# Attention's end in a four-part transformer kernel: column sums, late decay weights, the last residual, the block's close

## The chip, the cores and the metric

One NeuronCore of a Trainium2 chip runs the whole program in one launch. The metric is device time of the program in microseconds (us), the median of several executions. The engines are named as in the profile: PE (TensorE, matmul) with PEld (its weight loads), DVE (VectorE), ACT (ScalarE), POOL (GpSimd) and SP (SyncE, which only issues DMAs here). "PEclk" is the granted clock of PE: 1.00 is 2.4 GHz, 0.50 is 1.2 GHz.

## What is computed

The reference has four residual steps over `x` of 4 x 512 x 512 (16 tiles of 128 tokens), float32:

1. `x += tanh(g0) * attention(layernorm(x), ctx, ctx)`, eight heads, scores and softmax over the context;
2. `x += tanh(g) * mixture of 8 experts, 2 per token` (gate, up with 512 columns, down);
3. `x += tanh(g) * layernorm(x + summary)`, where `summary` is the mean over time of a linear recurrence over the context: `s_t = K s_(t-1) + W_in c_t + b_in`, then `W_out s + b_out`, with `K = sigmoid(decay)`. Since all of it is linear, the kernel weights each context row with a scalar (the decay weights, one per position, from a scan of 512 numbers), sums the rows per batch (`u`, 512 numbers for each of 4 batches), and multiplies by `W_in` and later `W_out`;
4. `x += tanh(g) * mixture of 64 experts, 4 per token, and two shared experts`.

The change is about the end of step 1, where `u` is also summed, and about the first lines of step 2.

## The kernel before, in words

The program consists of four blocks, one after the other; between two blocks all engines meet. `attention` is the first, `mixture0` the second. Within a block each engine has its own instruction stream, in program order, and semaphores tie them.

**Attention** runs a software pipeline over tiles (`steps`): step `i` does the scores of tile `i` in four quarters `b`, the rough maxima of tile `i+1` (bank `pM`), the attention output and residual of tile `i-1`, the gate logits of tile `i-2` (`xnT`, `wg`) and the places of tile `i-3` in its experts' tables (`positions`: PE L578, L579; `place`: DVE). The first and last steps are unrolled. For tile `i-1` the relay is: value matmuls (PE L543), copies of the sums `attn` (ACT L639, L640), reciprocals (DVE L754), product with `numer` (POOL L448), a `pool.drain()`, residual add into `x_sb` (POOL L450), statistics (DVE L769), scale factors (POOL L462 to L469), normalised tile `xn` (ACT L665), transposes (PE L603), `xnT` (ACT L648), gate logits (PE L609), the two largest and `mask` (DVE L708 to L723), positions, slots (DVE L737), scatter into the table `tab0` (POOL L426, indirect DMA).

**Decay weights.** In the first step DVE makes the scan `crow` (`state_weights`, L686), PE turns it to columns (L485, eight records for four matmuls) and flips it (L488), DVE copies it (`ccol`) and makes `wsel` (L695), weights of 4 columns per tile. PE waits for all that ahead of its first rough score. **Context sum.** For each of 16 context tiles one matmul has `wsel` (4 columns) as weights and 512 columns of context moving: `u` comes out as a row for each batch (`pM[0:4]`). The tiles are spread over steps 16 to 18 (L496); after the last, ACT copies the row (L671), PE turns it to columns (L517), ACT copies it to `ucol` (L673). Tiles 4 to 15 share one semaphore, so PE waits at tile 4 for all twelve loads, which SP issues (L358) when the last scores are done (`qk_done`). `W_in` (`win`, L369) comes behind them.

**Tail.** After the last place PE counts (L503), DVE makes the padding rows (`padrow`, L790), a table of tiles per expert (`tinfo`), then the rows of results (`take0`, L818 to L828) and the bias (`bin_col`). Eight padding writes of zeros, 256 KB each, go out after `padrow`: four by SP, two by ACT (L301), two by POOL (L432, indirect). The block closes with GpSimd's drain, as blocks do by default.

**Mixture 0.** SP waits for all zeroing, padding and scattering, reads the first row of a tile from `tinfo` and issues `m_x` (L900). PE first projects `ucol` by `W_in` in row form (L990: weights of 4 columns, 512 moving), DVE copies the row, PE turns it (L985), and DVE adds the bias into `mstate` (L1063), read only by the third block. Then, per expert tile: transposes (L949), ACT rounds (L1017), DVE makes the low part (L1059), PE multiplies up (L956, high and low parts: three matmuls for each block), and so on through ACT, DVE and POOL splits of the weights (L1002, L1044, L935).

Of the kernel before, what the change touches and what calls it, by code (L numbers as in the profile page):

```python
# [8 lines left out]
I32 = mybir.dt.int32  # L9
# [5 lines left out]
P = 128  # L15
# [20 lines left out]
SUMS = 2  # L36
AT_ONCE = 1
# [38 lines left out]
def build(nc, A, out):  # L76
    ctx = ExitStack()
    with ctx:
# [28 lines left out]
        chosen1 = sb("chosen1", [P, E1], BF16)  # L107

# [10 lines left out]
        with arena0:  # L119
# [4 lines left out]
            s_padded_too = ctx.enter_context(nc.semaphore("table0_padded_too"))  # L124
# [46 lines left out]
def attention(nc, A, T):  # L171
# [6 lines left out]
    with c:  # L178
# [41 lines left out]
        flip = xnT[:, 0, :]  # L220
# [3 lines left out]
        crow = attn[0:1, :]  # L224
        wsel = sb("wsel", [P, B, TPB, B])
        urow = sb("urow", [B, D])

        padf, padrow = sb("padf", [P, E0]), sb("padrow", [P, E0], I32)
        cnt, ntf, nti = sb("cnt", [P, E0]), sb("ntf", [P, E0]), sb("nti", [P, E0], I32)
# [3 lines left out]
        usum = sb("usum", [P, 4 * TILES])  # L233
        big = sb("big", [P, L0_TILES * E0])
        past = big[0:1, 0:L0_TILES * E0].rearrange("p (t e) -> p t e", e=E0)
        slots = usum[:, 2 * TILES:4 * TILES]
# [16 lines left out]
        ctx_loaded = [sem(f"ctx_loaded_{n}") for n in range(2)]  # L253
# [18 lines left out]
        wsel_ready = sem("wsel_ready")  # L272
        urow_ready, uT_full = sem("urow_ready"), sem("uT_full")

        block = c.enter_context(nc.Block())
# [28 lines left out]
        def _(sp):  # L304
# [68 lines left out]
        def _(pool):  # L373
# [8 lines left out]
            nc.gpsimd.memset(flip, 0.0)  # L382
            nc.gpsimd.memset(ones[:], 1.0)
            nc.gpsimd.memset(invt[:], 1.0 / SEQ)
            nc.gpsimd.memset(wsel[:], 0.0)
# [9 lines left out]
            nc.gpsimd.affine_select(flip, flip, [[1, P]], ALU.not_equal, 1.0, base=1 - P, channel_multiplier=1)  # L395
# [25 lines left out]
            for i in range(-3, TILES + 3):  # L421
# [57 lines left out]
        def _(pe):  # L479
# [3 lines left out]
            pe.wait_ge(crow_ready, 1)  # L483
            for j in range(TPB):
                last = nc.tensor.matmul(pM[:, j:j + 1], crow[0:1, j * P:j * P + P], ones[0:1, 0:1], start=True, stop=True)  # L485
            last.then_inc(col_full, 1)
            pe.wait_ge(col_ready, 1)
            nc.tensor.matmul(pM[:, 0:TPB], flip, ccol[:, 0, :], start=True, stop=True).then_inc(col_full, 1)  # L488
            pe.wait_ge(wsel_ready, 1)
# [17 lines left out]
            def weights_sum():  # L507

                for j in range(TPB):
# [4 lines left out]
            def context_columns():  # L514
                pe.wait_ge(urow_ready, 1)
                for n in range(DB):
                    last = nc.tensor.transpose(pM[:, n * B:n * B + B], urow[:, n * P:n * P + P], ident[0:B, 0:B])  # L517
                last.then_inc(uT_full, 1)
# [34 lines left out]
            def step(i, u, odd):  # L553
                s, o = odd, 1 - odd
                if valid(i):
                    need(pe, q_split, i + 1)
                    need(pe, k_lo_ready, i + 1)
                for b in range(4):
                    if valid(i):
                        scores(i, s, b)  # L560

# [13 lines left out]
                    if b == 0 and valid(i - 3):  # L575

                        need(pe, mask_ready, i - 2)
                        nc.tensor.matmul(pT[:, 0:E0], before[:], mask[:, o, :], start=True, stop=False)  # L578
                        nc.tensor.matmul(pT[:, 0:E0], onesb[:], chosen[:, o, :], start=False,  # L579
                                         stop=True).then_inc(pos_full, 1)  # L580
                        if isinstance(i, int) and i == TILES + 1:
                            weights_sum()
                            weighted_context(range(6, 9))
# [7 lines left out]
                    if isinstance(i, int) and (i, b) == (TILES, 1):  # L591
                        weighted_context(range(0, 2))
                    if isinstance(i, int) and (i, b) == (TILES, 3):
                        weighted_context(range(2, 6))
                    if isinstance(i, int) and (i, b) == (TILES + 1, 1):
                        weighted_context(range(9, 10))
# [1639 lines left out]
```

## Time and profile before

| | us |
|---|---|
| median of 3 runs | 1121.69 (1120.41 to 1123.66) |
| profiled execution, its own time | 1124.97 |
| its span in the profile | 1123.2 |
| attention, up to the meeting of the engines | about 0 to 324 |
| mixture 0 | about 324 to 533 |
| mean granted clock of PE | 0.967 |

Busy shares over the span: PE 92%, PEld 66%, DVE 64%, POOL 52%, ACT 45%. They are means over very different stages: in the last 30 us of attention no engine is busy throughout. In a row of the timeline, the first number is the start, the second the time from the start of the group to its end; the bracket is the idle time of the engine before it and what ended it. A float32 matmul appears as two MATMUL records, a float32 transpose as one. A row with "SPq" or "ACTq" is the issuing of DMAs, not their transfer.

### The profile page before, as it was taken

The numbers are of one execution on the slowest core, as the hardware profiler recorded it, in microseconds if no ns is written. First come the engines' busy times: TensorE is split into PE (matmuls) and PEld (weight loads), VectorE is DVE, ScalarE is ACT, GpSimd is POOL, SyncE is SP. The second block draws the span as 40 slices with busy tenths as digits, with TensorE's granted clock in tenths as the row PEclk, the third lists the DMA queues.
The fourth block names the chain that finished last, engine by engine and source line by source line (L and its number), as shares of the span: only waits on it lengthen the run. The fifth ranks groups of instructions, "written<-read, shape, count | busy, mean of one in ns | idle before, by whom it ended". The sixth has DMA issues, their size and how long they took to land. (4 is left out here: it accounts for less than half of the span.)

```text
span 1123.2 us, 18838 instructions
## 1 busy us (share of the span) xinstructions
PE 1028.6 (92%) x5364; PEld 739.4 (66%) x5364; DVE 723.4 (64%) x1703; ACT 500.6 (45%) x880; POOL 589.3 (52%) x556
## 2 busy tenths in 40 slices
PE   5899999999869999998899999999989999999950
PEld 3456555565327777775289478577768888888840
DVE  4577787876448888886688248267316666666650
ACT  3466566565338888886432201311313333333320
POOL 6466766775416676675534646356432344333541
PEclk8999999999989999999899999999999999999985
DMA  9976555773544332332540241043269999999638
GB/s 289 342 228 201 171 180 191 240 246 104 197 150 152 111 105 102 112 103 75 181 144 20 87 140 44 11 136 112 87 209 345 333 323 313 277 331 336 160 70 149
DMA packets 128254, 199.49 MB, mean 178 GB/s; under 512 B 35975, under 2 KB 44167, under 8 KB 128186
## 3 DMA queue, kind: packets, MB, share of 16 engines
q1 hardware_dynamic: 106538, 160.66, 42.7%
q0 software_dynamic: 21360, 37.48, 13.2%
q8 instruction: 32, 0.52, 0.2%
q10 hardware_dynamic: 288, 0.52, 0.1%
q14 instruction: 36, 0.29, 0.1%
HBM read 133.10 MB, written 87.56 MB: 196 GB/s over the span
## 5 line engine op out<-in xcount | busy, mean ns | idle before, releaser
L935 POOL TENSOR_TENSOR m_down_lo<-wo,m_down_hi 128x512 fp32r<-128x512 f32 x78 | 129.8, 1683 | 74.9 <-ACT m_down_hi L1030 74.9
L543 PE MATMUL bank<-win,vT 128*128 128x512 f32 x256 | 124.5, 600 | 0.0
L703 DVE TENSOR_REDUCE negmax<-bank 128x1 bf16<-128x512 f32 x128 | 85.6, 672 | 43.2 <-PE bank L550 42.8
L633 ACT ACTIVATE win<-bank 128x512 f32<-128x512 f32 x128 | 69.4, 594 | 90.1 <-PE bank L535 86.3
L1044 DVE TENSOR_TENSOR m_up_lo<-w,m_up_hi 128x1024 fp32r<-128x1024 f32 x78 | 96.8, 1242 | 13.1 <-ACT m_up_hi L1002 11.8
L2034 POOL DMA_INDIRECT out<-m_y,m_token x32 | 50.9, 1590 | 91.2 <-DMA out<-m_y,m_token 61.5
L1264 POOL DMA_INDIRECT tab<-stage_up,slot x64 | 65.9, 1029 | 53.4 <-DVE slot L1610 35.5
L2064 PE MATMUL bank<-y,m_w 128*128 128x128 f32 x736 | 89.7, 275 | 0.0
L2178 ACT ACTIVATE sh_gate_a<-bank 128x512 f32<-128x512 f32 (+1 forms) x40 | 20.5, 513 | 150.8 <-PE bank L2171 120.6
L2034 POOL DMA_INDIRECT sums<-m_y,m_token x32 | 51.2, 1599 | 69.2 <-DVE m_y L2128 41.3
L2064 PEld LDWEIGHTS bank<-y,m_w 128*128 128x128 f32 x736 | 86.4, 193 | 0.1
L2171 PE MATMUL bank<-flat_hi,w_hi 128*128 128x512 f32 (+1 forms) x320 | 74.4, 355 | 2.4 <-DVE flat_lo L1677 1.6
L550 PE MATMUL bank<-k_hi,q_parts 128*128 128x512 f32 x128 | 68.9, 549 | 7.7 <-issue 2.9
L2082 PE MATMUL bank<-split_space,m_h_hi 128*128 128x512 f32 x128 | 73.7, 576 | 1.9 <-DVE split_space L2114 1.9
L2171 PE MATMUL bank<-flat_lo,w_hi 128*128 128x512 f32 (+1 forms) x320 | 73.2, 350 | 1.6 <-issue 1.6
L2171 PE MATMUL bank<-flat_hi,w_lo 128*128 128x512 f32 (+1 forms) x320 | 71.9, 347 | 0.0
L956 PE MATMUL bank<-m_up_hi,m_xT_hi 128*128 128x512 f32 x156 | 67.7, 434 | 2.8 <-DVE m_up_lo L1044 2.6
L2092 ACT COPY y<-bank 128x512 f32<-128x512 f32 x64 | 37.4, 587 | 73.4 <-PE bank L2056 64.7
L543 PEld LDWEIGHTS bank<-win,vT 128*128 128x128 f32 x256 | 47.8, 192 | 27.1 <-issue 18.9
L754 DVE RECIPROCAL attn<-attn 128x128 f32<-128x128 f32 (+1 forms) x48 | 58.5, 1220 | 6.6 <-ACT attn L640 2.6
L956 PE MATMUL bank<-m_up_lo,m_xT_hi 128*128 128x512 f32 x156 | 61.6, 395 | 0.0
L956 PE MATMUL bank<-m_up_hi,m_xT_lo 128*128 128x512 f32 x156 | 61.3, 393 | 0.0
(297 smaller groups left out, 2503.9 us busy)
## 6 DMA issues: line engine op xcount, KB each, us to landing
tab<-zeros SPq DMA_DIRECT2D x16, 1056.0 KB
m_w<-in_L_ffn_Wg SPq DMA_DIRECT2D x46, 256.0 KB
m_w<-in_L_ffn_Wu SPq DMA_DIRECT2D x46, 256.0 KB
m_w<-in_L_ffn_Wd SPq DMA_DIRECT2D x46, 256.0 KB
m_x<-tab SPq DMA_DIRECT2D x39, 256.0 KB, 2.6
ytab<-m_y SPq DMA_DIRECT2D x39, 256.0 KB, 2.1
stage_up<-tab SPq DMA_DIRECT2D x32, 264.0 KB
m_x<-tab SPq DMA_DIRECT2D x32, 264.0 KB
```

What stands on the lines that cost most here:

```text
L543: nc.tensor.matmul(pO[s * 2 + h][:], vT[:, s, sb_, h:h + 2, :].rearrange("p a c -> p (a c)"), probs[:, sb_ % 2, h, :], start=(sb_ == 0), s ...
L550: nc.tensor.matmul(rough_bank(k, m)[:], q_parts[:, s, h, t * P:t * P + P], k_hi[:, s, h, :], start=True, stop=True).then_inc(pm_full, 1)
L633: nc.scalar.activation(probs[:, b % 2, h, :], pS[h][:], ACT.Exp, scale=1.0 / HEAD).then_inc(p_ready, 1)
L703: nc.vector.tensor_reduce(negmax[:, s, m:m + 1], rough_bank(k, m)[:], AX.X, ALU.max, negate=True).then_inc(pm_read, 1)
L935: nc.gpsimd.tensor_tensor(dn_lo[:, m, :], row(wo0, e * MB + m), dn_hi[:, m, :], ALU.subtract).then_inc(dn_lo_ready, 1)
L956: last = nc.tensor.matmul(pH[s][:], x[:, s, d, :], w[:, d, :], start=(d == 0 and part == 0), stop=(d == DB - 1 and part == 2))
L1044: nc.vector.tensor_tensor(up_lo[:, at, :], blocks(w01, e * DB + half * HALF, HALF), up_hi[:, at, :], ALU.subtract).then_inc(up_lo_ready, 1)
L1264: nc.gpsimd.indirect_dma_start(T["tab1"], bass.IndirectOffsetOnAxis(slot1[:, j, k:k + 1], 0), flat[:, j, :], None, bounds_check=E1 * CAP1 ...
L2034: nc.gpsimd.indirect_dma_start(tables[e % SUMS], bass.IndirectOffsetOnAxis(token[:, e % META:e % META + 1], 0), y[:, e % RING, :], None, b ...
L2064: last = nc.tensor.matmul(pH[s][:, k * CAP1:(k + 1) * CAP1], w[:, b, :], xT[:, s, b, :], start=(b == 0), stop=(b == DB - 1))
L2082: last = nc.tensor.matmul(pY[o][:], a[:, o, :], w[:, o, :], start=(part == 0), stop=(part == 2))
L2171: last = nc.tensor.matmul(out, w[:, k, wc], x[:, d, cols], start=(d == 0 and part == 0), stop=(d == DB - 1 and part == 2))
```

## The change

- The decay weights are made late: the scan (`state_weights`) at the end of DVE's step 14, the turning on PE in step 15 (`decay_column` behind the scores of quarter 1, `turned_column` behind the scores of quarter 3, each ahead of that quarter's value matmuls), the copies at the end of DVE's step 15 (`decay_columns`). `wsel` goes.
- The context is the stationary operand: for each context tile four pairs of 128-column weights and one moving column `ccol`, into columns of `pM`, so `u` comes out as columns. Loads are waited for four tiles at a time. The order over the last steps is 0-1, 2-7, 8, 9-10, 11-15 where it was 0-1, 2-5, 6-8, 9, 10-12, 13-15; `weights_sum` stands before tile 0; `positions` comes first in its quarter in the late steps.
- The projection by `W_in` is done in columns too (`project`): output columns 0 and 1 at the end of attention, 2 and 3 at the start of mixture 0. The copy and the transposes between go.
- The residual of tile 15 is added by DVE; POOL signals after its product, without a drain.
- POOL's two padding writes go to ACT, behind its copy of `ucol`; all eight count on one semaphore. The block is closed with `no_gpsimd_drain=True`.
- `take0` is computed at the end of mixture 0's DVE stream, `bin_col` ahead of the last `place`.

```diff
-        block = c.enter_context(nc.Block())
+        block = c.enter_context(nc.Block(no_gpsimd_drain=True))
...
-                    sp.dma_start(ctx_at[t], c_v[:, t, :]).then_inc(ctx_loaded[min(n, 1)], 16)
+                    sp.dma_start(ctx_at[t], c_v[:, t, :]).then_inc(ctx_loaded[n], 16)
...
-                if i == TILES + 2:
-                    pool.wait_ge(pad_ready, 1)
-                    for e in range(6, E0):
-                        nc.gpsimd.indirect_dma_start(T["tab0"], bass.IndirectOffsetOnAxis(padrow[:, e:e + 1], 0),
-                                                     zeros[:, 0:D], None).then_inc(T["s_padded_too"], 16)
...
-                        nc.gpsimd.tensor_tensor(attn[:, cols_], attn[:, cols_], numer[:, cols_], ALU.mult)
-                    pool.drain()
-                    nc.gpsimd.tensor_tensor(x_sb[:, i - 1, :], x_sb[:, i - 1, :], attn[:],
-                                            ALU.add).then_inc(x1_ready, 1)
+                        last = nc.gpsimd.tensor_tensor(attn[:, cols_], attn[:, cols_], numer[:, cols_], ALU.mult)
+                    if i == TILES:
+                        last.then_inc(x1_ready, 1)
+                    else:
+                        pool.drain()
+                        nc.gpsimd.tensor_tensor(x_sb[:, i - 1, :], x_sb[:, i - 1, :], attn[:],
+                                                ALU.add).then_inc(x1_ready, 1)
...
+            def turned_column():
+
+                pe.wait_ge(col_ready, 1)
+                nc.tensor.matmul(pM[:, 0:TPB], flip[:], ccol[:, 0, :], start=True, stop=True).then_inc(col_full, 1)
...
-                    if t in (0, 4):
-                        pe.wait_ge(ctx_loaded[t // 4], 16 * (TILES - 4) if t else 64)
-                    last = nc.tensor.matmul(pM[0:B, :], wsel[:, t // TPB, t % TPB, :], ctx_at[t],
-                                            start=(t == 0), stop=(t == TILES - 1))
+                    if t % 4 == 0:
+                        pe.wait_ge(ctx_loaded[t // 4], 64)
+                    for n in range(DB):
+                        at = n * B + t // TPB
+                        last = nc.tensor.matmul(pM[:, at:at + 1], ctx_at[t][:, n * P:n * P + P],
+                                                ccol[:, 1, t % TPB:t % TPB + 1],
+                                                start=(t == 0 and n == 0), stop=(t == TILES - 1 and n == DB - 1))
...
+                late = isinstance(i, int) and i >= TILES
                 for b in range(4):
                     if valid(i):
                         scores(i, s, b)
+                    if late and b == 0 and valid(i - 3):
+                        positions(i, o)
+                    if isinstance(i, int) and (i, b) == (TILES - 1, 1):
+                        decay_column()
+                    if isinstance(i, int) and (i, b) == (TILES - 1, 3):
+                        turned_column()
...
-            weighted_context(range(13, TILES))
-            context_columns()
+            weighted_context(range(11, TILES))
+            first_projections()
...
-            nc.scalar.copy(urow[:], pM[0:B, :]).then_inc(urow_ready, 1)
-            act.wait_ge(uT_full, 1)
-            nc.scalar.copy(ucol[:].rearrange("p n b -> p (n b)"), pM[:, 0:DB * B])
+            nc.scalar.copy(ucol[:].rearrange("p n b -> p (n b)"), pM[:, 0:DB * B]).then_inc(T["ucol_ready"], 1)
+            pad(act, range(6, 8))
...
+                            if isinstance(i, int) and i == TILES:
+                                nc.vector.tensor_tensor(x_sb[:, i - 1, :], x_sb[:, i - 1, :], attn[:], ALU.add)
+                                dve.drain()
...
-                if isinstance(i, int) and i == -3:
+                if isinstance(i, int) and i == TILES - 2:
                     state_weights()
+                if isinstance(i, int) and i == TILES - 1:
+                    decay_columns()
...
+def project(nc, T, columns):
+
+    out, win, ucol = T["bank"][6], T["win"], T["ucol"]
+    for m in columns:
+        for n in range(DB):
+            last = nc.tensor.matmul(out[:, m * B:m * B + B], win[:, n, m * P:m * P + P], ucol[:, n, :],
+                                    start=(n == 0), stop=(n == DB - 1))
+    return last
...
-            pe.wait_ge(T["s_win"], 16)
-            for n in range(DB):
-                last = nc.tensor.matmul(pY[0][0:B, :], ucol[:, n, :], winT[:, n, :], start=(n == 0), stop=(n == DB - 1))
-            last.then_inc(mrow_full, 1)
+            project(nc, T, range(EARLY_COLUMNS, DB)).then_inc(mstate_full, 1)
```

## Rows read from the trace of the kernel before

**Rows 1.** section 1 of the page: engine, busy us (share) x instructions

```profile
PE 1028.6 (92%) x5364; PEld 739.4 (66%) x5364; DVE 723.4 (64%) x1703; ACT 500.6 (45%) x880; POOL 589.3 (52%) x556
```

**Rows 2.** timeline, start: us, length, engine line op out<-in xcount [idle before <-releaser]

```profile
7.92 1.23 DVE L686 TENSOR_TENSOR_SCAN attn<-kdec,invt 1x512 f32<-1x512 f32 x1
...
9.29 1.83 PE L485 MATMUL bank<-ones,attn 1*128 1x1 f32 x8 [9.29 <-DVE attn L686]
...
13.98 4.12 PE L550 MATMUL bank<-k_hi,q_parts 128*128 128x512 f32 x8 [2.01 <-DVE wsel L695]
...
41.93 1.14 ACT L659 CAST k_hi<-wout 128x512 fp32r<-128x512 f32 x2 [5.63 <-DMA wout<-in_ctx]
```

**Rows 3.** timeline, last full steps of attention

```profile
279.25 0.17 DVE L729 TENSOR_TENSOR rows<-bank,base 128x8 f32<-128x8 f32 x1 [1.21 <-PE bank L579]
...
288.58 3.65 PE L543 MATMUL bank<-win,vT 128*128 128x512 f32 x8
...
289.91 0.17 DVE L723 TENSOR_TENSOR mask<-onehot 128x8 bf16<-128x8 f32 x1
```

**Rows 4.** timeline, the relay after the last value matmul

```profile
293.53 3.83 DVE L754 RECIPROCAL attn<-attn 128x256 f32<-128x256 f32 x3 [0.33 <-ACT attn L640]
...
298.94 0.17 DVE L723 TENSOR_TENSOR mask<-onehot 128x8 bf16<-128x8 f32 x1
...
301.83 1.26 POOL L450 TENSOR_TENSOR x_sb<-x_sb,attn 128x512 f32<-128x512 f32 x1 [3.68 <-issue]
...
303.19 0.69 DVE L769 BATCH_NORM_STATS2 bn<-x_sb 128x6 f32<-128x512 f32 x1 [4.09 <-POOL x_sb L450]
...
305.63 0.81 ACT L665 ACTIVATE xn<-x_sb,ln 128x512 f32<-128x512 f32 x1 [10.25 <-POOL ln L469]
...
308.47 0.66 PE L603 MATMUL bank<-ident,xn 128*128 128x128 f32 x4
...
313.67 0.18 PE L578 MATMUL bank<-mask,before 128*128 128x8 bf16 x1
...
315.35 0.17 DVE L790 CAST padrow<-padf 128x8 int32<-128x8 f32 x1
```

**Rows 5.** timeline from pads to first expert matmul; landing of L900

```profile
316.49 4.69 SPq L301 DMA_DIRECT2D tab<-zeros  x4
...
324.94 6.52 SPq L900 DMA_DIRECT2D m_x<-tab  x5
...
329.73 0.66 PE L949 MATMUL bank<-ident,m_x 128*128 128x128 f32 x4
...
331.78 0.50 PE L956 MATMUL bank<-m_up_hi,m_xT_hi 128*128 128x512 f32 x1 [0.22 <-DVE m_xT_lo L1059]
...
DMA to landing us min/median/max: 2.5/2.8/3.0
```

**Rows 6.** windows: length, busy by engine, PEclk, DMA share, GB/s

```profile
323.50:324.00 0.50, 0.00 (x0) 0.00 (x0) 0.00 (x0) 0.00 (x0) 0.00 (x0) 0.50 0.43 156
...
324.00:330.00 6.00, 5.95 (x10) 1.12 (x11) 2.53 (x3) 3.48 (x4) 0.37 (x4) 0.63 0.49 147
```

**Rows 7.** timeline, one-column records (L510) and row-form context (L496)

```profile
304.81 0.97 PEld L510 LDWEIGHTS bank<-ones,ccol 128*128 128x128 f32 x8
...
305.80 2.74 PE L496 MATMUL bank<-ctx_late,wsel 128*4 128x512 f32 x6
```

**Rows 8.** chain of waits, experts: start, length, what

```profile
844.02 3.57 PE bank L2064 x16
...
848.07 1.79 PE bank L2064 x16
```

**Rows 9.** windows, before the end of the first mixture

```profile
529.00:530.00 1.00, 0.90 (x3) 0.49 (x3) 0.00 (x0) 0.00 (x0) 0.05 (x1) 0.90 0.21 78
```

**Rows 10.** timeline, end of the first mixture

```profile
530.22 0.59 ACT L1034 COPY m_y<-bank 128x512 f32<-128x512 f32 x1 [2.58 <-PE bank L978]
...
533.34 5.21 PE L1316 MATMUL bank<-summary,mstate 128*4 128x512 f32 x8 [3.15 <-PEq L850]
```

More of the change, by code:

```diff
@@ L36 @@
 SUMS = 2
+EARLY_COLUMNS = 2
 AT_ONCE = 1
@@ L252, in attention @@
         var_ready, ln2_ready, xn_ready = sem("var_ready"), sem("ln2_ready"), sem("xn_ready")
-        ctx_loaded = [sem(f"ctx_loaded_{n}") for n in range(2)]
+        ctx_loaded = [sem(f"ctx_loaded_{n}") for n in range(TILES // 4)]
         ctx_summed, ln_done = sem("ctx_summed"), sem("ln_done")
@@ L381, in _ @@
             nc.gpsimd.memset(chosen[:], 0.0)
-            nc.gpsimd.memset(flip, 0.0)
+            nc.gpsimd.memset(flip[:], 0.0)
             nc.gpsimd.memset(ones[:], 1.0)
             nc.gpsimd.memset(invt[:], 1.0 / SEQ)
-            nc.gpsimd.memset(wsel[:], 0.0)
             nc.gpsimd.memset(power[:], -0.5)
@@ L481, in _, with decay_column @@
             pe.wait_ge(s_small, SMALL)
[L483 to L489, printed above, removed]
+            def decay_column():
+                pe.wait_ge(crow_ready, 1)
+                for j in range(TPB):
+                    last = nc.tensor.matmul(pM[:, j:j + 1], crow[0:1, j * P:j * P + P], ones[0:1, 0:1], start=True, stop=True)
+                last.then_inc(col_full, 1)
+            def turned_column():
+                pe.wait_ge(col_ready, 1)
+                nc.tensor.matmul(pM[:, 0:TPB], flip[:], ccol[:, 0, :], start=True, stop=True).then_inc(col_full, 1)
             def weighted_context(tiles):
                 for t in tiles:
-                    if t in (0, 4):
-                        pe.wait_ge(ctx_loaded[t // 4], 16 * (TILES - 4) if t else 64)
-                    last = nc.tensor.matmul(pM[0:B, :], wsel[:, t // TPB, t % TPB, :], ctx_at[t],
-                                            start=(t == 0), stop=(t == TILES - 1))
+                    if t % 4 == 0:
[5 more added lines that the diff above has]
+                                                start=(t == 0 and n == 0), stop=(t == TILES - 1 and n == DB - 1))
                 if t == TILES - 1:
@@ L512, in weights_sum, with first_projections, positions @@
                 last.then_inc(sum_full, 1)
-            def context_columns():
-                pe.wait_ge(urow_ready, 1)
-                for n in range(DB):
-                    last = nc.tensor.transpose(pM[:, n * B:n * B + B], urow[:, n * P:n * P + P], ident[0:B, 0:B])
-                last.then_inc(uT_full, 1)
+            def first_projections():
+                pe.wait_ge(T["s_win"], 16)
+                pe.wait_ge(T["ucol_ready"], 1)
+                project(nc, T, range(EARLY_COLUMNS))
+            def positions(i, o):
+                need(pe, mask_ready, i - 2)
+                nc.tensor.matmul(pT[:, 0:E0], before[:], mask[:, o, :], start=True, stop=False)
+                nc.tensor.matmul(pT[:, 0:E0], onesb[:], chosen[:, o, :], start=False,
+                                 stop=True).then_inc(pos_full, 1)
             def scores(i, s, sb_):
@@ L575, in step @@
                     if b == 0 and valid(i - 3):
[L577 to L583, printed above, removed]
+                        if not late:
+                            positions(i, o)
                         if isinstance(i, int) and i == TILES + 2:
@@ L691, in state_weights @@
                 for j in range(TPB):
-                    nc.vector.tensor_copy(ccol[:, 1, j:j + 1], pM[:, TPB - 1 - j:TPB - j])
-                dve.drain()
-                for b in range(B):
-                    last = nc.vector.tensor_copy(wsel[:, b, :, b], ccol[:, 1, :])
-                last.then_inc(wsel_ready, 1)
+                    last = nc.vector.tensor_copy(ccol[:, 1, j:j + 1], pM[:, TPB - 1 - j:TPB - j])
+                last.then_inc(decay_ready, 1)
             def rough_max(k, s, m):
@@ L745, in step @@
                 for m in range(8):
+                    if m == 0 and isinstance(i, int) and i == TILES + 2:
+                        summed_bias()
                     if m == 0 and valid(i - 3):
```

95 lines of the change are left out of this document (42 added, 53 removed).

## The prediction

> **What bounds the kernel now.** I read the page first: one core, TensorE (PE) busy 92% of the span [rows 1]. The chain of waits reaches back only to 842 us and lies in the experts, nearly all of it PE groups like [rows 8], which the change does not touch. The later stages start where attention and the first mixture leave off, so what an earlier stage loses or wins I carry to the end in full. So I went to the timeline around the places the diff names: the start, attention's last tiles, the two block ends, and to the windows for clock and DMA.
>
> The start: PE waits 2.01 us until 13.98 for `wsel`. But ScalarE stands idle 5.63 us until 41.93 for the keys of tile 2, a DMA that SyncE issues behind its own queue of loads [rows 2].
>
> Attention's end is no longer PE-bound; it is a relay. VectorE's reciprocals end at 297.36; GpSimd multiplies until 298.15, then starts nothing for 3.68 us, and adds the residual at 301.83; VectorE takes its statistics at 303.19; ScalarE's normalised tile ends at 306.44, but its transposes start at 308.47, behind six row-form context matmuls; positions of tile 15 start at 313.67; the padding rows are ready at 315.52 [rows 4]. SyncE issues pads to 321.18, the DMA engines carry them until about 323.75, everybody starts the next block at about 324.0, and SyncE issues the first expert tile at 324.94; PE, busy with the row-form projection nearly until 330, transposes that tile only then, and the first expert matmul starts at 331.78 [rows 5, 6].
>
> **Part by part**, along that relay; times are those of the profiled execution (span 1123.2, its own time 1124.97).
>
> *Decay weights out of the start.* PE can start earlier by no more than its 2.01 us of waiting, and GpSimd's chain too, whose statistics are queued behind the decay work. The cover is the key load that ScalarE awaits until 41.93: SyncE's queue does not depend on any of this, so I take 0; the ends are 0 and -2.0 [rows 2].
>
> *Decay weights into steps 14 and 15.* VectorE gets the scalar work after step 14: a scan of 1.23 us and two small operations, 1.7 us [rows 2]. It has 1.21 us free before tile 12's positions at 279.25, so about 0.5 us show: PE's transposes wait for that read [rows 3]. PE gets eight more pass records at (15, 1): 1.0 us by L510's eight [rows 7], in a stretch where PE is continuously busy. At (15, 3) the flip matmul stands in PE's queue after the scores (288.57, now 290.1) and waits for a copy that VectorE does only after its whole step 15, whose last result, `mask`, is at 290.08 before, and about 290.95 with the delays above. So PE waits to 291.3, and 0.25 for the flip itself: the value matmuls end at 295.2, not 292.2. Price +3.0 us; queued behind it are the values, ScalarE's copies of `attn`, the reciprocals. The ends are +1.5 (only the pieces of work) and +3.5.
>
> *Context by columns.* 16 tiles x 4 blocks x 2 records, each with 128-column weights and one moving column. L510 is this shape: 0.97 us for eight [rows 7]; so 0.97 a tile and 15.5 us in all, against 0.86 a tile and 13.8 us for the row form. It is dearer on PE and takes away only the turning of a row into columns. Where it lies matters more. Six tiles (2 to 7) lie in PE's gap: logits of tile 14 end at about 300.0, the block ends at about 305.8; PE used to wait there for all twelve loads at once and now waits for four tiles at a time, so I charge no wait. Nothing stands now between positions and the transposes of tile 15, which saves what stood there. At L485, in the start, the same kind of matmul took 0.23 a record instead of 0.12 [rows 2, 7]: that is the rival below. In the chain of waits one and the same group of 16 (L2064) takes 3.57 us at the low clock and 1.79 at the high one [rows 8].
>
> The Trainium skill ("TensorE: Matmul & The Clock Gate", Part 4) says that transposes do not count as PE work for the clock in the way matmuls do. If one-column matmuls were treated so, the sum would be that of the rival; by the trace neither is decided, since its one-column stretches last 1 us with wide matmuls around them.
>
> *Residual on VectorE.* GpSimd's drain goes from this place. Before: 297.36 to 303.19, 5.83 us. After: VectorE's choice for tile 14 lies in between (its `mask` ends at 299.11, 1.75 after the reciprocals), then an add, 0.7 (a 128x512 operation of VectorE takes 0.69), and 0.2 around it: 2.65 us [rows 4]. Gain 3.2; the drain before the scale factors comes 3 us later than the scatters it may have waited for, so I charge nothing (bound: 1 us).
>
> *Sum to the pads.* Statistics start at 303.19 + 3.0 - 3.2 = 303.0, the normalised tile ends at about 306.2; transposes at 306.35 instead of 308.47 (2.1 gained). One context tile and the logits: positions 311.05 instead of 313.67 (three tiles of row form stood ahead, 2.6 us; now two of column form, 1.94, beside 1.75 of VectorE): 2.6 gained. `summed_bias`, two small operations, fits into VectorE's wait for them. Pads ready at 312.9.
>
> *To the end of the block.* Five context tiles end at 316.05, ScalarE copies `ucol` (0.2), eight early projections (1.94) end at 318.35. SyncE's four pads are issued from 313.85 to 318.55 at its old pace; ScalarE's pads 6 and 7, new there and behind `ucol`, to about 318.9 (1.2 each, the pace of SyncE's four in 4.69 us). The last pad lands 2.5 later, as before (321.2 to 323.75 [rows 6]), at 321.0. The block without GpSimd's drain closes at about 319.3: at the next block end ScalarE's last copy ends at 530.81, its store must be issued and land (2.5), and PE starts the next block at 533.34 [rows 10], so little is left for the closing itself. But SyncE's first act is still to wait for all eight pads, and then to read a register, 0.95 us as before: first expert tile issued at 321.9, 3.0 gained. GpSimd's two pads are gone, from an idle engine. If the drain had been all, this term would be nil: the pads' landing held both.
>
> *First expert tile.* Before 324.94 to 331.78, 6.84. Now it lands 2.8 after issue [rows 5], 324.7; the late projections (319.3 to 321.3) are over; transposes, rounding, low part take 2.05 as before (329.73 to 331.78): 326.8. Gain 5.0 so far. Then the clock: in the old kernel PE idled before 324, and the projection ran at 0.63 of the clock in the mean, partly at the low level (1.2 GHz), so that the experts began at the high one (2.4 GHz) [rows 6]. Now PE idles from 321.3 to 324.7 and nearly until 326.8; the fall comes after a like gap, and the expert matmuls themselves run low. The first twelve take about 2.8 us at the high level (PE's up half for tile 0, by the timeline 331.78 to 334.6); the low one doubles such a group, as it does L2064's [rows 8], less what waiting hides: about 2.4 us more, and ScalarE's and VectorE's splits wait for them. I take +2.4; ends 0 and +4.
>
> *Results' rows moved* behind the first mixture: seven small operations of VectorE, about 2 us, there beside the last down matmuls, copy and store until 533.3 [rows 10]: nothing; without this cover 2 us.
>
> Sum: 0 + 3.0 - 3.2 - 2.4 (transposes and positions) - 0.4 (pads) - 2.0 (projection) + 2.4 = -2.6 us. 1124.97 - 2.6 = 1122.4 for the profiled execution; that one lies 3.3 above the median of the runs, 1121.69, so the median to expect is 1119.1. The parts' own ends give 1115 to 1123.5.
>
> **Rivals.**
> *The clock falls under the column form (slower).* From 295.2 on PE runs transposes, weights sum, context, logits, projections, all with 1 to 8 moving columns, where it used to have 512-column matmuls. For it: L485 took 0.23 a record; the granted clock began to fall in a microsecond in which PE was 90% busy, after some sparse ones [rows 9]. Against: L510's eight ran at the high pace, though for 1 us [rows 7]. Price, if it falls at about 298: a tile costs 1.8 instead of 0.97. Context tiles 1 to 7 and the logits: +6 at positions of tile 14; tile 8, logits, 9 and 10: +3.5; 11 to 15: +4; early projections +1.6, of which the pads hide little, since ScalarE's two wait for `ucol`. Less 1 to 2 of waits that are filled. `ucol` at about 330, pads landed at 334.7, first expert matmul at 340.7: 8.9 late instead of 5.0 early, and +2.4 for the low start: 11.3, or 1133. It decides from where the low level holds through more than about three context tiles.
> *The gain is kept whole (faster).* If the first expert tiles are paced by the splits and not by PE (PE waits at the first expert matmul for VectorE's low part, 2.05 us after it began the transposes [rows 5]), the low clock costs nothing: 1116.7; with the flip's wait also short, 1115.
> *It does not do what it says.* If GpSimd's hold is not the drain but the multiply's end, VectorE's add waits as long: 3.2 back, 1122.3.
>
> **Chances.** Forecast (column form at the high clock, low start of the experts, 1119) 0.42; clock falls 0.38; kept whole 0.13; no gain from the residual 0.07. 0.3% is 3.4 us, about what this measurement tells from no change. The forecast's own range is 1116 to 1122, and a quarter of it is beyond 3.4 us. Faster 0.24, within 0.36, slower 0.40. The range for all, 1115 to 1135, reaches the slower case; the middle between 1123 and 1129 is thin.
>
> **What would show it.** The start: PE's first rough score at about 13.75 and ScalarE's `k_hi` of tile 2 still at about 41.9. Late decay: PE idle 1 to 1.5 us before the flip matmul, released by VectorE's copy. Residual: VectorE's statistics within 3 us of the last reciprocal, no long gap on GpSimd. Context: eight records in 0.97 us and a granted clock of 1.00 from 298 to 318; 1.8 and 0.50 would be the rival. Block: first expert load issued at 321.9, about 2 us after the other engines start. Experts: the first L956-like matmuls at 0.43 and the clock back within a tile or two. The prediction is wrong if the clock is low in the context tiles, or if the first expert matmul is not 4 to 6 us earlier.

## The result, and the profile after

The change makes the kernel slightly slower: 1124.93 us, median of 20 executions (1119.76 to 1128.42), beside 1120.81 for before in 20 (1116.12 to 1125.51); ratio 1.0036, interval [1.0023, 1.0050], +4.1 us. The forecast was 1119.1, and slower stood in the text as a rival with 0.38.

The profiled execution of after took 1123.86, span 1122.1, less than that of before, but not by the change: after is 5.9 us late at 637 and 2.0 early at 866, and the code between is the same. So I compare stretches. One stretch holds everything that was changed in the tail and what follows from it: from ScalarE's exponential in step 14 (272.09 before) to its last copy in mixture 0 [rows 10]. It lasts 258.1 us before and 261.9 after (+3.8). In this text it is called **the stretch**. A second profile of before has 262.4 for it (below), so the stretch serves to find where time goes; how much the change costs is told by the medians.

Section 1 of the page of after, as in [rows 1]: PE is busy 9.7 us more, and PEld 29.5, though what was added on PE would take some 2 us at the high clock (an estimate from [rows 7]: 15.5 us of column form for 13.8 of row form).

```profile
PE 1038.3 (93%) x5476; PEld 768.9 (69%) x5476; DVE 721.5 (64%) x1699; ACT 500.0 (45%) x879; POOL 583.9 (52%) x552
```

Where it comes from shows in the windows of after (start:end, length, busy us of PE, PEld, DVE, ACT, POOL, then PEclk, DMA share, GB/s):

```profile
296.00:300.00 4.00, 4.00 (x38) 3.98 (x36) 2.43 (x2) 3.01 (x5) 2.20 (x3) 1.00 1.04 316
300.00:308.00 8.00, 8.00 (x41) 8.00 (x40) 4.26 (x15) 0.81 (x1) 1.86 (x5) 0.52 0.81 313
308.00:312.00 4.00, 3.74 (x21) 3.66 (x20) 0.70 (x7) 0.59 (x1) 0.79 (x1) 0.50 0.00 0
336.00:341.00 5.00, 4.92 (x13) 3.66 (x13) 1.46 (x3) 1.22 (x3) 0.00 (x0) 0.50 0.40 124
341.00:346.00 5.00, 4.30 (x21) 3.35 (x20) 3.67 (x6) 4.04 (x7) 1.89 (x2) 0.97 0.00 0
```

PE has no idle time from 296 to 308, its weight loads neither, and yet the granted clock goes to 0.50 (1.2 GHz) at about 300.4 (0.52 over the 8 us from 300) and stays there until about 341, behind the first 512-column matmuls of the experts. What PE did before it fell: since the last value matmul (it ends at 296.2) transposes, the sum of the weights, one-column context matmuls and the logits of tile 14 (eight columns).

The timeline of after, from step 14 to the first experts (rows answering to [rows 3 to 5]; x is the number of records joined in a row):

```profile
280.01 1.21 DVE L695 TENSOR_TENSOR_SCAN crow<-kdec,invt 1x512 f32<-1x512 f32 x1
292.12 0.39 PE L486 MATMUL bank<-ccol,flip 128*128 128x4 f32 x2 [0.39 <-DVE ccol L701]
297.27 1.93 PE L495 MATMUL bank<-ccol,wout 128*128 128x1 f32 x16
297.48 3.82 DVE L765 RECIPROCAL attn<-attn 128x256 f32<-128x256 f32 x3 [2.19 <-ACT attn L650]
302.98 6.97 PE L495 MATMUL bank<-ccol,ctx_late 128*128 128x1 f32 x32
302.99 0.69 DVE L781 TENSOR_TENSOR x_sb<-x_sb,attn 128x512 f32<-128x512 f32 x1
303.76 0.69 DVE L783 BATCH_NORM_STATS2 bn<-x_sb 128x6 f32<-128x512 f32 x1
306.35 0.81 ACT L675 ACTIVATE xn<-x_sb,ln 128x512 f32<-128x512 f32 x1 [7.02 <-POOL ln L462]
310.26 1.12 PE L613 MATMUL bank<-ident,xn 128*128 128x128 f32 x4 [0.26 <-DVE rows L738]
317.85 0.17 PE L524 MATMUL bank<-mask,before 128*128 128x8 bf16 x1
317.96 8.67 PE L495 MATMUL bank<-ccol,ctx_late 128*128 128x1 f32 x40
319.52 0.17 DVE L806 CAST padrow<-padf 128x8 int32<-128x8 f32 x1
326.67 0.17 ACT L681 COPY ucol<-bank 128x16 f32<-128x16 f32 x1 [14.67 <-PE bank L495]
327.34 1.38 ACTq L297 DMA_DIRECT2D tab<-zeros  x2
331.78 4.91 SPq L910 DMA_DIRECT2D m_x<-tab  x5
337.01 0.79 PE L965 MATMUL bank<-m_up_hi,m_xT_hi 128*128 128x512 f32 x1
343.17 0.47 PE L965 MATMUL bank<-m_up_hi,m_xT_hi 128*128 128x512 f32 x1 [0.70 <-DVE m_up_lo L1044]
535.48 0.59 ACT L1034 COPY m_y<-bank 128x512 f32<-128x512 f32 x1 [2.46 <-PE bank L987]
```

Read it for the record counts. Sixteen records took 1.93 us (0.97 for a tile of eight) before 299; 32 records took 6.97 from 302.98 on: 1.74 a tile. The normalised tile is ready at 307.16, its transposes start at 310.26, behind context tiles that should have been done. The relay of the residual works as hoped: last reciprocal ends at 301.30, statistics start at 303.76. ScalarE's last two pads wait for `ucol`, at 326.67, and the first load of an expert tile (331.78) waits for them. The first expert matmul is 5.2 us late against [rows 5], and the last copy 5.3.

### The profile page after: what moved, and what is told of

The parts are those of the page before. It is cut to its first block and busy times, and to the rows that moved or that the text cites. A ratio compares the mean times of both kernels' runs of the same rounds, so it can differ in the third digit from the quotient of the medians.

```text
span 1122.1 us, 19068 instructions
## 1 busy us (share of the span) xinstructions
PE 1038.3 (93%) x5476; PEld 768.9 (69%) x5476; DVE 721.5 (64%) x1699; ACT 500.0 (45%) x879; POOL 583.9 (52%) x552
## 5 line engine op out<-in xcount | busy, mean ns | idle before, releaser
L558 PEld LDWEIGHTS bank<-k_hi,q_parts 128*128 128x128 f32 x128 | 25.3, 199 | 59.7 <-DVE negmax L712 36.6
L421 POOL DMA_INDIRECT tab<-xn,slot x32 | 32.9, 1027 | 57.9 <-DVE slot L746 53.0
```

The lines of the kernel that those rows point to most:

```text
L558: nc.tensor.matmul(rough_bank(k, m)[:], q_parts[:, s, h, t * P:t * P + P], k_hi[:, s, h, :], start=True, stop=True).then_inc(pm_full, 1)
```

## Experiments

Time is the median of an experiment's executions; the level of before differed between groups of kernels run together (1120.09 beside the kernels with row form, early weights, both, and two idle matmuls; 1129.66 beside four idle matmuls, first series, and the kernels with GpSimd's residual and with its drain; 1127.18 for the rest), so I compare ratios to it; 0.01 of it is 11.2 us. "Stretch" is that of the profiled execution.

| kernel | time, us | ratio to before | stretch, us |
|---|---|---|---|
| before | 1120.81 | 1 | 258.1 |
| after (columns, late weights) | 1124.93 | 1.0036 [1.0023, 1.0050] | 261.9 |
| row form, late weights | 1113.05 | 0.9936 [0.9914, 0.9958] | 252.4 |
| columns, early weights | 1122.71 | 1.0017 [1.0001, 1.0034] | 259.3 |
| row form, early weights | 1110.06; again 1115.88 | 0.9918 [0.9892, 0.9944]; 0.9895 [0.9874, 0.9917] | 249.0; 250.0 |
| after + 2 idle matmuls a tile | 1134.49 | 1.0132 [1.0105, 1.0158] | 270.7 |
| after + 4 idle matmuls a tile | two groups, below | faster group, second series: 1.0017 [0.9996, 1.0039] | 261.5; 284.1 |
| row, early, GpSimd's residual | 1123.02 | 0.9954 [0.9933, 0.9974] | 254.8 |
| row, early, drain and GpSimd's pads | 1121.70 | 0.9937 [0.9916, 0.9958] | 252.1 |
| row, early, early projection | 1117.70 | 0.9918 [0.9896, 0.9940] | 251.1 |

**Undo the column form alone.**

```diff
-                    for n in range(DB):
-                        at = n * B + t // TPB
-                        last = nc.tensor.matmul(pM[:, at:at + 1], ctx_at[t][:, n * P:n * P + P],
...
+                    last = nc.tensor.matmul(pM[0:B, :], wsel[:, t // TPB, t % TPB, :], ctx_at[t],
+                                            start=(t == 0), stop=(t == TILES - 1))
```

(with `wsel`, the row's copy and turning, and the row-form projection at the start of mixture 0, as before)

> The kernel after, with the context sum and the projection by W_in put back into row form (the decay-weight columns are still made late; all else as after). Theory A (the one-column matmuls let the granted clock of PE fall; after shows 0.50 from 301 to 341 while PE is busy throughout): clock 1.00 from 298 to 318, transposes of tile 15 at 307.3 instead of 310.3, positions of tile 15 at about 312 instead of 317.9, first expert matmul at about 328.5 instead of 337.0, time about 1117 (1115 to 1119). Rival B (the clock falls there whatever the matmuls' shape, because the stretch is sparse; the form only changes the work): 0.50 in the row form too, with 1.7 a context tile, time 1123 or more. Rival C (the loss is the late decay weights and the start): time 1123 to 1125, whatever the clock does.

Measured: 1113.05; by the ratios 11.2 us under after, 9.5 in the stretch. Its window, its context tiles 4 to 7, and three rows that answer to 310.26, 317.85 and 337.01 above:

```profile
300.00:308.00 8.00, 6.28 (x23) 1.91 (x23) 5.36 (x22) 0.81 (x1) 2.71 (x6) 1.00 0.82 314
302.25 3.60 PE L497 MATMUL bank<-ctx_late,wsel 128*4 128x512 f32 x8
307.70 0.63 PE L614 MATMUL bank<-ident,xn 128*128 128x128 f32 x4 [1.72 <-ACT xn L676]
312.08 0.18 PE L525 MATMUL bank<-mask,before 128*128 128x8 bf16 x1
328.32 0.50 PE L973 MATMUL bank<-m_up_hi,m_xT_hi 128*128 128x512 f32 x1 [0.22 <-DVE m_xT_lo L1076]
```

The clock stays at 1.00, though PE now idles 1.7 us there. B is out, and so is C as the cause of the whole loss; the gain is larger than A's 8 us, and 1113.05 lies below its range. One doubt stays: the row form changes the work too. The next two kernels leave the one-column work as it is.

**Keep the clock up with idle matmuls.**

```diff
+                    for _ in range(2):
+                        nc.tensor.matmul(pO[0][:], before[:], identb[:].unsqueeze(1).broadcast_to([P, 4, P]), start=True, stop=True)
```

> The kernel after, with two idle matmuls behind every context tile (bf16, 128x512, into a bank nobody reads): 32 more matmuls, 6.8 us of PE at the high clock, and nothing taken away. Theory A (what lets the clock fall is that only one column moves for each weight load): the clock stays at 1.00 from 298 on, a context tile with its two fillers costs 1.40 (0.97 + 0.43) instead of 1.75 for the tile alone, the pads come about 2 to 3 us earlier, time 1121 to 1123: more work and less time. Rival B (the clock falls anyway): tile and fillers 2.6 at the low clock, 13 us more of PE from 298 to 326, time 1134 or more. Rival C (clock irrelevant, the work counts): 1130.

Measured: 1134.49, rival B's number. Two did not hold it; tile and fillers take 2.38 from start to start (1.57 and 0.80), and PEclk is 0.61, then 0.50:

```profile
300.00:308.00 8.00, 8.00 (x43) 7.07 (x44) 4.14 (x15) 0.81 (x1) 1.72 (x5) 0.61 0.76 293
308.00:328.00 20.00, 19.74 (x89) 16.72 (x90) 5.32 (x35) 0.58 (x1) 3.96 (x4) 0.50 0.12 45
301.91 1.71 PE L495 MATMUL bank<-ccol,wout 128*128 128x1 f32 x8
303.48 1.01 PE L499 MATMUL bank<-identb,before 128*128 128x512 bf16 x2
```

That fits B, or an A for which two are too few; four of them tell. For four, A gave a clock of 1.00 from 298 to 325, 1.82 us for a tile with its idle matmuls, the first expert matmul at about 338, and 1123 to 1127 us.

> The kernel after, with four idle matmuls behind every context tile instead of two (64 in all, 13.6 us of PE at the high clock). Two were too few: the clock was 0.50 from about 303 on, and the time 9.6 above the kernel after. [...] Rival B (the clock falls in this stretch whatever PE is given): tile with fillers 3.4, the end of the context sum 26 us later, 1148 or more.

> The kernel with four idle matmuls behind every context tile once more. Its profile was as theory A says (clock 1.00 from 290 to 328, 0.95 and 0.86 us for tile and fillers, the first mixture as early as in the kernel after), but its four timed runs scattered from 1128 to 1156 beside a kernel before of 1123 to 1135. If the profile is typical: 1122 to 1127 beside 1120 for before, that is 3 to 5 us slower than before and no slower than the kernel after. If idle matmuls cost something that the profiled run did not show (a clock held back elsewhere): 8 us or more over the kernel before, with a lower mean clock.

Measured: the executions of this one kernel fall into two groups, with nothing between. In the second series, beside 1127.18 for before, six of fourteen lie at 1127.08 to 1129.37 and eight at 1151.66 to 1156.36. In the first series, beside 1129.66, the four are 1127.58, 1133.23, 1150.70 and 1155.77. Each group was profiled once. The execution of 1133.23 us, first series:

```profile
300.00:308.00 8.00, 8.00 (x61) 6.37 (x61) 4.64 (x15) 0.81 (x1) 2.28 (x5) 1.00 0.81 309
308.00:328.00 20.00, 19.74 (x149) 15.33 (x147) 6.83 (x41) 0.76 (x2) 3.96 (x4) 1.00 0.35 132
303.66 0.95 PE L495 MATMUL bank<-ccol,wout 128*128 128x1 f32 x8
304.47 1.02 PE L499 MATMUL bank<-identb,before 128*128 128x512 bf16 x4
```

and that of 1151.66 us, second series:

```profile
300.00:308.00 8.00, 8.00 (x33) 6.22 (x32) 4.16 (x15) 0.10 (x1) 1.76 (x5) 0.50 0.77 297
308.00:328.00 20.00, 19.74 (x89) 14.29 (x88) 1.88 (x16) 1.30 (x2) 2.04 (x2) 0.59 0.07 27
302.71 1.85 PE L495 MATMUL bank<-ccol,wout 128*128 128x1 f32 x8
304.41 1.87 PE L499 MATMUL bank<-identb,before 128*128 128x512 bf16 x4
```

The same instructions take half the time or the whole: stretch 261.5 or 284.1. Where the clock held, PE did 64 more matmuls than after in the same stretch (261.9). And in the faster group of the second series this kernel, at 1.0017 of before, is no slower than after at 1.0036. So the price is the clock's and not the order's or the work's. With none or two idle matmuls a tile the clock fell near 300 in all three profiled executions, with four in one of two. B, a fall whatever PE is given, is out; A stands, but its times for four hold for one group of executions only.

**Decay weights early again.**

```diff
-                if isinstance(i, int) and i == TILES - 2:
-                    state_weights()
-                if isinstance(i, int) and i == TILES - 1:
-                    decay_columns()
+                if isinstance(i, int) and i == -3:
+                    state_weights()
+                    decay_columns()
```

(on PE `decay_column` and `turned_column` ahead of the first rough score, with a wait for `decay_ready`)

> The kernel after, with the decay-weight columns made in the first step again, as before (PE waits for them ahead of its first rough score). Theory: the late decay weights cost twice. In step 15 the value matmuls end 2.3 us later by them; and the start they free gives nothing at 41.9 us, where everybody waits for the keys of tile 2, but PE then idles longer and comes out at the low clock (after: 0.83 from 40 to 60, before 1.00), 1.3 us. Both come back: 1121.3 (1120 to 1123), with the offset of after against before gone by 60 us, and the clock still 0.50 from 300 to 340. Rival: what is saved in step 15 is lost again in the low-clock stretch, whose PE work is then in front anyway, and the start was chance: 1124 to 1125.

> Both: row form and decay weights at the start; of the change are left the residual of tile 15 on VectorE, the pads on SyncE and ScalarE, the close without GpSimd's drain, the loads waited for by four tiles, positions first in their quarter, and the moved small work. If the two causes add (8 for the form and its clock, 3.5 for the late weights): 1113.5 (1112 to 1116). If the late weights' price was only visible because the step was late anyway: same as the run with row form alone, 1117. If the other edits give nothing: 1121, as before.

> Row form and early decay weights again, as the best so far, beside the kernel with the early projection: 0.992 of the kernel before, as at first (0.989 to 0.994), whatever the level of this chip.

Measured: by the ratios late weights cost 2.1 us with columns and 2.0 with rows (3.0 by the medians, 1113.05 to 1110.06), neither clear of the intervals; in the stretch 2.6 and 3.4. The profiles have the place: from the start of the stretch the last reciprocal ends after 27.8 us in both kernels with late weights and after 25.4 in both with early ones. They add to the column form, whose price by the ratios is 11.2 with late weights and 11.1 with early ones (12.7 by the medians, 1122.71 to 1110.06). Row form and early weights together came out below the range given for them (1110.06 for 1112 to 1116); their 0.9895 in the last series lies inside its range. The second half of the first expectation was wrong: with early weights the clock from 40 to 60 was 0.74, not 1.00, and the offset had not gone. So before itself had to be profiled again, for the start.

> The kernel before, profiled once more, for the start. In the first profile the keys of tile 2 were there at 41.9 and PE worked at 1.00 from 40 to 60; in the five kernels since they came between 42.5 and 44.0 and the clock was 0.74 to 0.83 there. If that is chance (the phase of the clock, the DMA queue), this profile shows a time between 42 and 44 or a low clock too, whatever the decay weights do. If it hangs on the changes, it is 41.9 and 1.00 again. The span of the first profile was also longer than most, by 6 to 8 us that were lost between 640 and 850, where nothing was changed: if that is chance, this one comes out at 1117 to 1120.

Measured, as one execution: 1136.07, above what was expected, so nothing is said here of the level. At the start the keys come late and the clock is low in before too; at attention's end a second thing shows:

```profile
43.75 1.14 ACT L659 CAST k_hi<-wout 128x512 fp32r<-128x512 f32 x2 [8.45 <-DMA wout<-in_ctx]
40.00:60.00 20.00, 15.00 (x61) 8.92 (x61) 10.65 (x16) 10.49 (x19) 8.02 (x11) 0.83 0.85 265
303.71 3.58 PE L496 MATMUL bank<-ctx_late,wsel 128*4 128x512 f32 x4 [3.59 <-DMA ctx_late<-in_ctx]
304.00:308.00 4.00, 4.00 (x10) 1.05 (x8) 1.45 (x8) 0.20 (x1) 2.26 (x4) 0.50 0.32 123
```

(The expectation has the keys between 42.5 and 44.0 in the five kernels; with two idle matmuls they were there at 41.70.) The 1.5 us by which after was late at step 14 are not the change's. Over all profiles step 14 (ScalarE's exponential) starts at 273.0 to 273.9 in the five with late weights and at 274.0 to 275.5 in seven with early ones, this one of before among them (274.32); only the first profile of before (272.09) lies outside. So late weights seem to give back about 1 us at the start, which the stretch leaves out and the ratios hold.

Before's wait for twelve loads at once is followed by a low clock in both profiles of before. In the first it was 3.66 us, and the low level held for 3.4 us, from about 301 to 304.5; here it was 3.59 us, and the low level held from about 302 to 312. These are the rows of the first:

```profile
301.45 3.39 PE L496 MATMUL bank<-ctx_late,wsel 128*4 128x512 f32 x4 [3.66 <-DMA ctx_late<-in_ctx]
300.00:304.00 4.00, 2.55 (x4) 0.35 (x4) 0.73 (x2) 0.00 (x0) 1.26 (x1) 0.64 0.84 328
304.00:308.00 4.00, 4.00 (x18) 1.45 (x16) 1.00 (x9) 0.81 (x1) 2.28 (x5) 0.94 0.00 0
```

The four row-form records take 0.85 us each there, and 0.46 each in [rows 7]. The stretch is 262.4 here and was 258.1: before's own varies by 4 us, as much as the whole difference to after. The three row-form kernels that wait for four loads at a time and keep VectorE's residual (row form with late weights, and with early ones twice) stay at 1.00 until 319.6 at least.

**GpSimd's residual back**, on row form and early weights:

```diff
-                    if i == TILES:
-                        last.then_inc(x1_ready, 1)
-                    else:
-                        pool.drain()
+                    pool.drain()
```

> Row form and early decay weights (1110.1), but the residual of tile 15 is added by GpSimd behind a drain, as before. Theory (the prediction's term): the last reciprocal ends at 300.5 and the statistics start 2.4 later there; with GpSimd 5.8 later, as before; everything behind it is one relay: 1113.5 (+3.4). Rival: GpSimd's wait was for the scatters in flight, which now start at another time, or the pads' landing is set by something else: 1110 to 1111.

Measured: 0.9954 beside 0.9918 and 0.9895, so 4.1 to 6.7 us; stretch +5.8 and +4.8. More than the relay's 3.4, because PE now waits longer for `xn`, and the clock falls behind that wait:

```profile
303.15 1.26 POOL L444 TENSOR_TENSOR x_sb<-x_sb,attn 128x512 f32<-128x512 f32 x1 [2.36 <-issue]
304.52 0.69 DVE L783 BATCH_NORM_STATS2 bn<-x_sb 128x6 f32<-128x512 f32 x1 [2.77 <-POOL x_sb L444]
304.00:308.00 4.00, 0.38 (x4) 0.25 (x4) 1.63 (x10) 0.81 (x1) 1.67 (x5) 1.00 0.45 171
308.00:312.00 4.00, 4.00 (x14) 2.04 (x14) 0.00 (x0) 0.59 (x1) 1.78 (x2) 0.54 0.37 135
```

The rival's price, 1110 to 1111, is out. What holds GpSimd in its drain stays open: before the add of tile 15 it is idle 2.36 us here and 3.68 and 3.54 in the two profiles of before, but behind the same drain 0.32 us for tile 14 (add at 285.55) and 1.84 for tile 13 (270.98).

**Drain and GpSimd's pads back**, on the same:

```diff
-        block = c.enter_context(nc.Block(no_gpsimd_drain=True))
+        block = c.enter_context(nc.Block())
...
-            pad(act, range(6, 8))
```

> Row form and early decay weights (1110.1), but the block is closed with GpSimd's drain and GpSimd writes pads 6 and 7, as before. Theory: first expert load unchanged against the ready padding rows (9.3 us behind them in both kernels, because SyncE waits for all pads' landing), but the block closes 1 to 2 us later, and the row-form projection, at the low clock, ends that much later, after the first expert tile has landed: +1.3, 1111.4. Rival 1: nothing (1110). Rival 2: the drain holds the block to the pads' landing and more, as at 324.0 before: +3, 1113.

Measured: 0.9937, 2.1 to 4.7 us; stretch +3.1 and +2.1, more than the 1.3 expected. The load is no later (321.58; 321.99 without the drain, 46.97 and 46.95 us from the start of the stretch), the block's first matmul is, by 1.3 us, and the projection then ends behind the tile's landing. Drain and pads were put back together, so what each costs is not shown:

```profile
320.64 6.10 PE L1011 MATMUL bank<-win,ucol 128*4 128x512 f32 x8 [4.40 <-PEq L180]
321.58 3.67 SPq L921 DMA_DIRECT2D m_x<-tab  x4
326.66 0.66 PE L970 MATMUL bank<-ident,m_x 128*128 128x128 f32 x4
```

**The projection into PE's wait at the block's end** (four row-form matmuls moved from mixture 0 to behind `context_columns()`):

```diff
             context_columns()
+            pe.wait_ge(T["ucol_ready"], 1)
+            for n in range(DB):
+                last = nc.tensor.matmul(pM[0:B, :], ucol[:, n, :], T["win"][:, n, :], start=(n == 0), stop=(n == DB - 1))
```

> Row form and early decay weights, and the row-form projection by W_in moved to the end of attention, into PE's wait for the block to close (there PE was idle from 316.5 to 319.8, and then projected at the low clock for 5.3 us, until 325.1, when the first expert tile had just landed at about 324.8). Theory: the projection takes 3.4 us there at the high clock, ends at about 320.3, the first transposes start when the tile lands, 0.3 to 1 us earlier, and the clock does not fall in front of the experts: 0.5 to 1.5 us under the run of row form and early weights beside it. Rival: the block now closes behind the projection, and SyncE's first load with it: no gain, or 0.5 slower.

Measured: 0.9918 beside 0.9895: 1117.70 and 1115.88, no gain; a loss of about 2 us, though the intervals overlap. The first row pair is this kernel, the second the one without the move, where the projection ran until 324.5:

```profile
324.90 1.12 PE L970 MATMUL bank<-ident,m_x 128*128 128x128 f32 x4 [4.00 <-DMA m_x<-tab]
328.02 0.63 PE L977 MATMUL bank<-m_up_hi,m_xT_lo 128*128 128x512 f32 x1
```
```profile
324.46 0.66 PE L965 MATMUL bank<-ident,m_x 128*128 128x128 f32 x4
326.86 0.40 PE L972 MATMUL bank<-m_up_hi,m_xT_lo 128*128 128x512 f32 x1
```

PE idles 4.00 us and starts the experts at the low clock (0.63 a record instead of 0.40). From the start of the stretch the first transposes are 0.6 us earlier and the first expert matmul 0.1, but the second half of the first tile is 1.0 later, and so is the last copy (1.1): ScalarE's split waits for PE's slow first half, VectorE's low part for the split, PE for that. Without the move the clock falls in PE's wait too (at 319.6), and the projection that follows, with 512 moving columns, is under way when it comes back (323.0), ahead of the experts. The work that I took for a nuisance had that use.

## Why the prediction failed, step by step

- *The step that failed is "context by columns": 0.97 us a tile and the logits, projections and transposes around it at the high clock.* It measured 1.74 a tile from 303 on. That was the slower rival, by name and place; I gave it 0.38 and the forecast 0.42, on the ground of eight records that had run for 1 us amid wide matmuls [rows 7]. A row of 1 us cannot tell what 16 us of the same do. The rival's own evidence was no better: L485's 0.23 a record stood behind 9.29 us of idle PE, and the 512-column records after it took 0.52 each too (0.23 apart at the high level), eight in 4.12 [rows 2], so it told of the place and not of the form. The rival came true by more than its reasons gave. The form costs 11.2 and 11.1 us in the runs (by the ratios), where the sum charged 1.7 more of PE time and took 2.0 off at the projection.
- The prediction quoted the Trainium skill ("TensorE: Matmul & The Clock Gate", Part 4), by which transposes do not count for the clock as matmuls do, and asked whether one-column matmuls are treated alike. By these traces a run of one-column matmuls does not hold the clock (0.50 from 300.4 on); what transposes alone do, no run here shows. Part 1 of that page ("What's actually happening") says that the clock follows how busy PE has been. Here PE and PEld are busy 8.00 of 8.00 us and the clock falls to 0.52, so busy time as the profile counts it does not hold it; the measurement decides.
- *The rival was overpriced*: 1133 for 1124.9. It had the fall at 298; it came at 300.4, so context tiles 0 and 1 and part of 2 went at the high clock. It had the first expert matmul 8.9 late; it was 5.2, of which 1.5 are the start's.
- *"I charge no wait" for the loads*: right in after (PE is never idle there), but what stood in its place in before was left out of the sum: a wait of 3.66 us and 3.4 us of low clock behind it.
- *Low clock at the experts, +2.4*: the row is there (0.43 apart until 341), the price is not. First matmul +5.23, tile 1 some 0.5 more, last copy +5.26: nothing is left at the end. But this is not a rule: with the early projection a low start of the experts went with +1.1 in the stretch. So "kept whole" was right in this term for after, and its reason, that PE's slowness is slack, does not hold in general.
- *Late decay weights, +3.0*: 2.4 at the reciprocals, 2.0 to 3.4 in time, which the intervals alone would not show. Right in place and about right in size, though the wait for the flip was 0.39, not 1 to 1.5.
- *Start, 0*: k_hi of tile 2 at 42.57 where about 41.9 was forecast. Over all profiles it stands at 41.7 to 42.6 with late weights and at 42.9 to 44.0 with early ones, the first profile of before (41.93) apart: rather a gain of about 1 us, inside the stated ends of 0 and -2.0.
- *Residual, -3.2*: reciprocals to statistics 2.46 us instead of 5.83 [rows 4]: 3.4. Right in place and size; the run that undoes it shows 4.1 to 6.7, with the clock's part that I had not seen.
- *Transposes and positions, -2.4*: lost to the low clock in after (3.1 us behind `xn`). With rows they start 0.14 behind `xn`, as forecast.
- *Block close*: in the row-form kernels the load comes 9.2 and 9.3 us behind the padding rows with and without GpSimd's drain and pads; what these delay is PE's first work in the next block. The forecast had both parts (-0.4, -2.0); 2.1 to 4.7 measured.
- In after the pads are not hidden beside the context sum, but behind it: ScalarE's two wait for `ucol`, and the first load comes 3.1 us behind the last of them (2.7 in the row-form kernels).

The version with row form and early weights beats both kernels: 0.9918 and 0.9895 of before in two series, 9 to 12 us. The residual (4.1 to 6.7) and the drain with the pads (2.1 to 4.7) account for much of that. What stays open: how much of the rest is the loads by four tiles and the order, which no run takes apart, although before's low clock behind its wait for twelve loads points at them; and why the form's price is larger by the ratios than in the stretch (11.2 and 11.1; 9.5 and 10.4).

## What to carry to other kernels

Turning a product so that the big operand is stationary and one column moves saves a transpose and looks free on PE's busy time. But here the clock fell in a run of such matmuls, and everything after it paid until the 512-column matmuls of the experts, behind which it came back. Price such a form at both clock levels before choosing, and take the row that lasts as long as the new stretch, not the shortest. And in a relay at a block's end, wide matmuls in a wait can be worth more than an empty PE (here by about 1 us, hardly clear of the noise). Profile the kernel before more than once: one stretch of it differed by 4 us between two profiles.

## What the runs showed of the hardware

- A granted clock of 0.52 with PE and its weight loads busy 8.00 of 8.00 us: no idle time is needed for a fall.
- One kernel with two times, about 1129 and 1154, and nothing between: in the two profiled executions the same matmuls run at 1.00 or at 0.50 from 300 us on.
- The kernel before, twice: behind idle waits of 3.66 and 3.59 us PE comes out at the low clock, for 3.4 us in one profile and for 10 in the other.
- GpSimd, behind a drain, starts its add for tile 15 2.4 to 3.7 us after its product (three profiles), for tile 14 0.3 us after; VectorE's add in its place starts 0.9 us after that product (1.7 after the last reciprocal).
